# Moving the casts and remainders of a three-way bf16 split to other steps of a software-pipelined attention kernel

## The chip, the cores and the metric

One core of one Trainium2 chip runs the whole kernel. The metric is the device time in microseconds (us); three runs gave 420.11, 420.8 and 423.27, median 420.8.

## What is computed

The input `x` is 8 batches of 512 tokens with 128 features. One transformer layer is applied:

```
x = layernorm(x + attention(x))          # 16 heads of 8 features, causal
x = layernorm(x + channel_mix(x))
# scores of one head, before the softmax
scores = alpha * tanh(q @ k.T / beta) + lam * (soft_bits @ soft_bits.T) / 2 \
         + (hexc @ M_h @ hexc.T) / 6 * 2 * sigmoid(scale)
soft_bits, hexc = tanh(x @ hex_w.T), tanh(x @ q6_w.T)      # 6 features each
# channel_mix: r = sigmoid(mix_r @ W_r.T); out = r * (relu(mix_k @ W_k.T)**2 @ W_v.T)
```

The products that make the scores run on TensorE in bf16. To keep float32 accuracy, each of their operands is split into three bf16 levels whose sum is the float32 value.

## The kernel before

**Periods and steps.** Work is written out by hand in periods, one for each batch `b`, and each period has 20 steps `t`. One step handles a pair of 128x512 score blocks. Five engines each have their own instruction list with the same steps, and they meet only at semaphores. For pair `t`, TensorE makes the raw scores (`scores`, L513), ScalarE takes the tanh (`tanh`, L777), TensorE adds the bias product (`biases`, L538), VectorE adds the two (`main`, L999, one step later), ScalarE takes the exponential three steps later (`exp`, L786), GpSimd zeroes what lies above the diagonal (`mask`, L882), and TensorE multiplies with the values (`weighted`, L557, at steps given by `VALUES_STEPS`). PSUM holds three pairs, so `scores(t)` waits until `main(t-3)` is done. I write main(9) for `main` of pair 9, which is VectorE's first instruction in step 10; mask(6) is `mask` of pair 6, GpSimd's first in step 9.

**Side work.** Within period `b`, two further batches are served. "Post" finishes batch `b-1`: normalising the attention output, the output projection, residual and layernorm, the channel mix and its layernorm. "Prep" makes the stacks of batch `b+2`: the transposed input, the projections Q and K, the features J (`feats`, made by ScalarE) and the mapped features G. The dictionaries `PREP` and `POST` of VectorE (L1113) and GpSimd (L935) say in which step each stage stands. An engine does its main instruction first, then the stages of `PREP`, then those of `POST`. Period 0 has prep and no post, periods 1 to 5 have both, periods 6 and 7 have post alone. What comes ahead of period 0 is written out separately.

**The split.** For each of Q, K, J, G, four instructions follow one another across two engines: `hi` (VectorE casts the float32 value to bf16, level 0), `rest` (GpSimd subtracts level 0), `mid` (VectorE casts the remainder, level 1), and `lo` (GpSimd subtracts level 1 and writes level 2). All work on tiles of 128x512. After `lo`, the SyncE queue writes the three levels to DRAM (`to_dram`, in the order Q, K, J, G, each after its own `lo`), and in the next period loads them back as stacks (`load_stacks`). `hi` of the next batch overwrites level 0 in `parts`, so it waits until the DRAM write of the batch before has landed (`scr_in`, L1037).

**The first layernorm of the post work.** In step 10 VectorE adds the residual (L1101), takes statistics (L1089) and moments (L1096). GpSimd then makes the inverse deviation in its step 10 (`inv_std`, L913 and L915) and normalises in step 11 (`norm`, L923 and L927). In between stands mask(8). TensorE's `weighted(7)` in step 13 needs mask(8), and its transpose of the normalised tile in step 14 (L598) needs `norm`.

Of the kernel before, what the change touches and what calls it, by code (L numbers as in the profile page):

```python
# [62 lines left out]
Q, K, J, G = range(4)  # L63
# [76 lines left out]
def build(nc, x, qkv_w, out_w, hex_w, lam_logit, q6_w, transforms, transform_weights, scale_logit,  # L140
# [17 lines left out]
    with ExitStack() as ctx:  # L158
# [181 lines left out]
        def lagged(b, t, lag):  # L340

            return (b, t - lag) if t >= lag else (b - 1, t - lag + PAIRS)
# [8 lines left out]
        def _(sp):  # L351
# [150 lines left out]
            for half, (_, bs, _) in enumerate(HALVES):  # L502
                sp.wait_ge(tail["final"], half + 1)
                sp.dma_start(out[B - 1].rearrange("(n p) c -> p n c", p=P)[:, bs], final[:, bs]).then_inc(stored, 16)
# [4 lines left out]
        def _(pe):  # L509
# [232 lines left out]
            for half, (blocks, _, _) in enumerate(HALVES):  # L742
                pe.wait_ge(tail["sums"], half + 1)
                transposes(tail_bank("sums_T", half), lambda n: sums_sb[:, 1, n * P:(n + 1) * P],
                           blocks).then_inc(tail["sums_T"], 1)
            for half, (blocks, _, _) in enumerate(HALVES):
                pe.wait_ge(tail["attn_first"], 1)
                pe.wait_ge(tail["attn"], half + 1)
                transposes(tail_bank("attn_T", half), lambda n: attn[:, n, :], blocks).then_inc(tail["attn_T"], 1)
# [118 lines left out]
        def _(pool):  # L868
# [13 lines left out]
            def mask(b, t):  # L882

                v, p = pair_probs(t), t % PAIRS_PER_QUAD
                if p < 4:
                    blocks = [v[:, :, 0:P]] + ([v[:, :, 3 * P:T]] if p >= 2 else [])
                else:
                    blocks = [v.rearrange("p u (r i) -> p (u r) i", r=2)[:, :, 0:P]]
                pool.wait_ge(exp_done, PAIRS * b + t + 1)
                stand_alone(pool)  # L890
                for v in blocks:
                    last = nc.gpsimd.affine_select(out=v, in_=v, compare_op=ALU.is_ge, fill=0.0, base=0,  # L892
                                                   pattern=[[0, v.shape[1]], [1, P]], channel_multiplier=-1)
                last.then_inc(mask_done, 1)
# [35 lines left out]
            def gated_residual(n):  # L930
# [1 line left out]
                pool.wait_ge(dve_freed, side_units.through(n + 1, "kv"))  # L932
                nc.gpsimd.tensor_tensor(res[:], gated[:], x1[:], ALU.add).then_inc(gate_done, 1)

            PREP = {6: [(rest, Q)], 10: [(lo, Q), (rest, K)], 13: [(lo, K), (rest, J)], 14: [(rest, G)],  # L935
                    16: [(lo, J)], 17: [(lo, G)]}
            POST = {10: [(inv_std, 0)], 11: [(norm, 0)], 18: [(gated_residual,)], 19: [(inv_std, 1), (norm, 1)]}

            def period(b, par, post, prep, last=False):
                for t in range(PAIRS):  # L940
                    if t >= EXP_LAG or post:
                        mask(*lagged(b, t, EXP_LAG))
                    for stage, *a in PREP.get(t, []) if prep else []:
                        stage(b + 2, *a)
# [40 lines left out]
        def _(dve):  # L985
# [78 lines left out]
            def sums_out(n, k):  # L1064

                dve.wait_ge(pv_done, PAIRS * n + (k + 1) * PAIRS // 2)
                v.tensor_copy(sums_sb[:, k, :], sums[:]).then_inc(sums_read, 1)
# [38 lines left out]
            def gate(n):  # L1106
# [3 lines left out]
                v.scalar_tensor_tensor(out=gated[:], in0=r_tanh[:], scalar=1.0, in1=o, op0=ALU.add,  # L1110
                                       op1=ALU.mult).then_inc(dve_freed, 1)

            PREP = {0: [(x_out,)], 2: [(projected, Q)], 3: [(projected, K)], 5: [(hi, Q)], 9: [(mid, Q), (hi, K)],  # L1113
                    11: [(mid, K), (hi, J)], 12: [(features_i,)], 13: [(hi, G)], 15: [(mid, J)], 17: [(mid, G)]}
            POST = {1: [(normalise, 0)], 6: [(normalise, 1)], 8: [(attn_out,)],
                    10: [(residual,), (stats, 0, 0), (stats, 0, 1), (moments, 0)], 14: [(x1_out,)],
                    18: [(gate,)], 19: [(stats, 1, 0), (stats, 1, 1), (moments, 1)]}
# [1 line left out]
            def period(b, par, post, prep, values=True):  # L1119
                parity[0] = par  # L1120
                for t in range(PAIRS):
# [4 lines left out]
                    if t == VALUES_STEPS[PAIRS // 2 - 1]:  # L1126
                        sums_out(b, 0)
                    for stage, *a in PREP.get(t, []) if prep else []:
                        stage(b + 2, *a)
# [230 lines left out]
```

## Time and profile before

| | |
|---|---|
| median of three runs | 420.8 us |
| profiled execution, its own time | 420.74 us |
| span of its trace | 418.8 us |
| mean granted TensorE clock | 0.985 |
| busy: PE, VectorE (DVE), ScalarE (ACT), GpSimd (POOL) | 368.2, 332.7, 327.3, 230.6 us |
| busy share of the span | 88%, 79%, 78%, 55% |
| VectorE `main` (L1004), 160 instructions | 202.8 us, mean 1274 ns |
| GpSimd `rest` (L899) and `lo` (L905) together, 60 instructions | 70.9 us |
| VectorE `hi` (L1038) and `mid` (L1043) together, 64 instructions | 36.5 us |

The busy shares are averages over the whole span. All four engines are well used, so what counts is which of them is waited for in which step. The trace is therefore read period by period. Period 3 of the kernel runs from about 175 to 219 us from the span's start, and periods 1 to 5 repeat nearly to the hundredth of a microsecond.

### The profile page before, as it was taken

To read this page: it belongs to the slowest core of one execution; us is meant where nothing else is said; L and a number is where in the kernel's file an instruction comes from. 1 tells how busy PE (TensorE), PEld (TensorE's weight loads), DVE (VectorE), ACT (ScalarE), POOL (GpSimd) and SP (SyncE) were. 2 spreads that over 40 slices of the span, in tenths; PEclk is the share of its full clock that TensorE was granted. 3 is DMA by queue.
4 is the path that set the end of the run, shared out by engine and by line. 5 is a ranking of instruction groups with operands and counts; after the bars stand their busy time and mean duration, and the time that the engine had idled before them with its cause. 6 is when DMAs were issued, how large, how long until landed. Compare 5 with 4: busy or idle time off the path is not lost.

```text
span 418.8 us, 8760 instructions
## 1 busy us (share of the span) xinstructions
PE 368.2 (88%) x2907; PEld 191.3 (46%) x2907; DVE 332.7 (79%) x539; ACT 327.3 (78%) x364; POOL 230.6 (55%) x367
## 2 busy tenths in 40 slices
PE   4557798899999999999899989999989998999863
PEld 1232343345455544645364535454544554345442
DVE  4873677988988989798979897989887958786643
ACT  1002389999998989799889989899989998999621
POOL 4313535834687359644965488646873446344532
PEclk9999999999999999999999999999999999899978
DMA  3354587786621775167624764276318610100000
GB/s 100 94 144 121 162 275 189 232 236 166 200 84 48 205 193 172 49 164 195 190 80 121 188 182 131 85 194 186 123 52 206 173 59 7 45 27 1 2 27 25
DMA packets 37807, 53.74 MB, mean 128 GB/s; under 512 B 3522, under 2 KB 35266, under 8 KB 36190
## 3 DMA queue, kind: packets, MB, share of 16 engines
q1 hardware_dynamic: 34078, 51.49, 43.4%
q10 hardware_dynamic: 3696, 1.84, 1.8%
q8 instruction: 18, 0.29, 0.3%
q14 instruction: 15, 0.12, 0.1%
HBM read 38.69 MB, written 14.61 MB: 127 GB/s over the span
## 4 chain that ended last, share of the span: by engine, by line
PE 50%; DVE 15%; issue 10%; POOL 9%; SPq 7%; ACT 5%; DMA 3%; ACTq 1%; POOLq 0%; DVEq 0%
PE raw L511 22%; PE side_bank L511 13%; PE sums L511 12%; DVE probs L1004 6%; ACT probs L788 3%; PE side_bank L598 3%; POOL probs L892 2%; SPq L401 2%; ACT probs L783 2%; POOL x L927 2%; POOL x L923 2%; SPq L415 2%; POOL parts L905 2%; SPq L412 2%; DVE bn L1089 1%
## 5 line engine op out<-in xcount | busy, mean ns | idle before, releaser
L1004 DVE SCALAR_TENSOR_TENSOR probs<-probs,scal,raw 128x1024 f32<-128x1024 f32 x160 | 202.8, 1274 | 40.4 <-PE raw L511 39.4
L783 ACT ACTIVATE probs<-raw 128x1024 f32<-128x1024 f32 x160 | 163.9, 1025 | 33.2 <-PE raw L511 32.2
L892 POOL TENSOR_SCALAR_AFFINE_SELECT probs<-probs 128x256 f32<-128x256 f32 (+1 forms) x224 | 98.9, 458 | 131.6 <-ACT probs L788 131.1
L788 ACT ACTIVATE probs<-probs 128x1024 f32<-128x1024 f32 x160 | 169.3, 1060 | 0.9 <-DVE probs L1004 0.9
L511 PE MATMUL raw<-q_stack,k_stack 72*128 72x384 bf16 (+3 forms) x512 | 99.0, 306 | 10.9 <-DVE probs L1004 6.9
L511 PE MATMUL raw<-i_stack,j_stack 111*128 111x384 bf16 (+3 forms) x512 | 98.1, 304 | 2.7 <-ACT probs L783 2.5
L511 PE MATMUL sums<-probs,values 128*32 128x256 f32 (+2 forms) x1280 | 93.3, 391 | 5.1 <-POOL probs L892 4.1
L511 PEld LDWEIGHTS raw<-q_stack,k_stack 72*128 72x128 bf16 x512 | 38.9, 99 | 63.8 <-DVE probs L1004 35.3
L511 PEld LDWEIGHTS raw<-i_stack,j_stack 111*128 111x128 bf16 x512 | 42.4, 99 | 48.6 <-issue 15.3
L511 PEld LDWEIGHTS sums<-probs,values 128*32 128x32 f32 x1280 | 29.8, 109 | 50.9 <-issue 27.2
L899 POOL TENSOR_TENSOR whole<-whole,parts 128x512 f32<-128x512 f32 x22 | 26.2, 1189 | 23.1 <-DVE parts L1038 23.1
L905 POOL TENSOR_TENSOR parts<-whole,parts 128x512 bf16<-128x512 f32 x30 | 35.1, 1171 | 4.2 <-DVE parts L1043 4.2
L1043 DVE CAST parts<-whole 128x512 bf16<-128x512 f32 x32 | 19.6, 612 | 2.9 <-POOL whole L899 2.8
L915 POOL TENSOR_TENSOR rstd<-var_eps,minus_half 128x4 f32<-128x4 f32 x14 | 14.7, 1047 | 1.2
L796 ACT ACTIVATE feats<-side_bank 128x512 f32<-128x512 f32 x8 | 4.9, 611 | 12.4 <-PE side_bank L511 12.4
L511 PEld LDWEIGHTS side_bank<-w_r_mix,x1T 128*128 128x128 f32 x112 | 13.6, 191 | 1.0
L511 PE MATMUL side_bank<-w_r_mix,x1T 128*128 128x128 f32 x112 | 13.6, 275 | 0.0
L511 PE MATMUL side_bank<-x1T,w_k_mix 128*128 128x512 f32 x28 | 13.2, 591 | 0.0
L835 ACT ACTIVATE probs<-shift_col 1x1536 bf16<-1x1536 bf16 x1 | 1.5, 1481 | 14.6 <-DVE w_r_mix L1244 14.6
L1038 DVE CAST parts<-whole 128x512 bf16<-128x512 f32 x24 | 12.3, 511 | 0.7 <-DMA q_rows<-parts 0.5
L1089 DVE BATCH_NORM_STATS2 bn<-res 128x6 f32<-128x128 f32 x56 | 12.2, 280 | 0.2
L511 PE MATMUL side_bank<-xT,wqT 128*128 128x512 f32 x14 | 9.7, 781 | 2.9 <-DVE xT L1019 2.3
(144 smaller groups left out, 347.6 us busy)
## 6 DMA issues: line engine op xcount, KB each, us to landing
q_stack<-q_rows SPq DMA_DIRECT2D x21, 384.0 KB
k_stack<-k_rows SPq DMA_DIRECT2D x21, 384.0 KB
i_stack<-lattice_i SPq DMA_DIRECT2D x21, 288.0 KB
i_stack<-hamming_i SPq DMA_DIRECT2D x21, 288.0 KB
q_rows<-parts SPq DMA_DIRECT2D x8, 384.0 KB, 8.7
k_rows<-parts SPq DMA_DIRECT2D x8, 384.0 KB, 3.0
lattice_i<-parts SPq DMA_DIRECT2D x8, 288.0 KB
k_rows<-parts SPq DMA_DIRECT2D x8, 256.0 KB, 3.3
```

The lines of the kernel that those rows point to most:

```text
L511: return nc.tensor.matmul(o, lhsT, rhs, start=start, stop=stop, **kw)
L598: last = nc.tensor.transpose(o[:, n * P:(n + 1) * P], src(n), ident[:])
L783: nc.scalar.activation(pair_probs(t), raw[:, t % PSUM_PAIRS, :].rearrange("p (u i) -> p u i", u=2), ACT.Tanh).then_inc(tanh_done, 1)
L788: nc.scalar.activation(pair_probs(t), pair_probs(t), ACT.Exp).then_inc(exp_done, 1)
L892: last = nc.gpsimd.affine_select(out=v, in_=v, compare_op=ALU.is_ge, fill=0.0, base=0, pattern=[[0, v.shape[1]], [1, P]], channel_multipli ...
L899: nc.gpsimd.tensor_tensor(whole[:, kind, :], feats[:] if kind == J else whole[:, kind, :], parts[:, kind, 0, :], ALU.subtract).then_inc(re ...
L905: nc.gpsimd.tensor_tensor(parts[:, kind, 2, :], whole[:, kind, :], parts[:, kind, 1, :], ALU.subtract).then_inc(lo_done[kind], 1)
L915: nc.gpsimd.tensor_tensor(rstd[:], var_eps[:], minus_half[:], ALU.pow).then_inc(rstd_done, 1)
L1004: v.scalar_tensor_tensor(out=o, in0=o, scalar=scal[:, 2:3], in1=raw[:, t % PSUM_PAIRS, :].rearrange("p (u i) -> p u i", u=2), op0=ALU.mult ...
L1038: v.tensor_copy(parts[:, kind, 0, :], feats[:] if kind == J else whole[:, kind, :]).then_inc(hi_done[kind], 1)
L1043: v.tensor_copy(parts[:, kind, 1, :], whole[:, kind, :]).then_inc(mid_done[kind], 1)
L1089: v.bn_stats(bn[:, blk, :], res[:, blk, :]).then_inc(bn_done, 1)
```

## The change

Nothing is added or taken out. Some stages stand at other steps. `hi` of K goes from step 9 to 5, of J from 11 to 6, of Q from 5 to 4. `mid` of Q goes from 9 to 8, of K from 11 to 9, of J from 15 to 12, of G from 17 to 16. On GpSimd `rest` of Q goes from 6 to 5, of K from 10 to 6, of J from 13 to 8; `lo` of Q from 10 to 9, of J from 16 to 14.

```diff
-            PREP = {6: [(rest, Q)], 10: [(lo, Q), (rest, K)], 13: [(lo, K), (rest, J)], 14: [(rest, G)],
-                    16: [(lo, J)], 17: [(lo, G)]}
+            PREP = {5: [(rest, Q)], 6: [(rest, K)], 8: [(rest, J)], 9: [(lo, Q)], 13: [(lo, K)],
+                    14: [(lo, J), (rest, G)], 17: [(lo, G)]}
...
-            PREP = {0: [(x_out,)], 2: [(projected, Q)], 3: [(projected, K)], 5: [(hi, Q)], 9: [(mid, Q), (hi, K)],
-                    11: [(mid, K), (hi, J)], 12: [(features_i,)], 13: [(hi, G)], 15: [(mid, J)], 17: [(mid, G)]}
+            PREP = {0: [(x_out,)], 2: [(projected, Q)], 3: [(projected, K)], 4: [(hi, Q)], 5: [(hi, K)], 6: [(hi, J)],
+                    8: [(mid, Q)], 9: [(mid, K)], 12: [(features_i,), (mid, J)], 13: [(hi, G)], 16: [(mid, G)]}
```

The code ahead of period 0 has its own order of the same stages and is left as it is.

## Rows read from the trace of the kernel before

**Rows 1.** The chain that ended last, whole span: start, us, what.

```profile
113.73 1.03 POOL x L923
291.72 1.02 POOL x L923
376.18 1.02 POOL x L923
```

**Rows 2.** Timeline of PE, 178 to 226 us: start, us, what, idle before.

```profile
201.37 0.61 PE L511 MATMUL raw<-q_stack,k_stack 72*128 72x384 bf16 x4 [0.41 <-DVE probs L1004]
...
202.98 0.85 PE L511 MATMUL sums<-probs,values 128*32 128x384 f32 x8 [0.56 <-POOL probs L892]
...
205.27 0.63 PE L598 MATMUL side_bank<-ident,x 128*128 128x128 f32 x4 [0.46 <-POOL x L927]
...
206.19 0.60 PE L511 MATMUL raw<-q_stack,k_stack 72*128 72x512 bf16 x2
```

**Rows 3.** Timeline of GpSimd (POOL), same stretch.

```profile
193.45 0.41 POOL L892 TENSOR_SCALAR_AFFINE_SELECT probs<-probs 128x256 f32<-128x256 f32 x1 [1.22 <-ACT probs L788]
195.97 0.66 POOL L892 TENSOR_SCALAR_AFFINE_SELECT probs<-probs 128x256 f32<-128x256 f32 x1 [2.11 <-ACT probs L788]
...
198.57 1.16 POOL L905 TENSOR_TENSOR parts<-whole,parts 128x512 bf16<-128x512 f32 x1
...
200.81 0.24 POOL L913 TENSOR_SCALAR var_eps<-mean_var 128x4 f32<-128x4 f32 x1
...
208.85 1.16 POOL L899 TENSOR_TENSOR whole<-whole,parts 128x512 f32<-128x512 f32 x1
209.97 1.67 POOL L892 TENSOR_SCALAR_AFFINE_SELECT probs<-probs 128x256 f32<-128x256 f32 x4
...
219.97 0.23 POOL L913 TENSOR_SCALAR var_eps<-mean_var 128x4 f32<-128x4 f32 x1 [1.21 <-DVE mean_var L1096]
```

**Rows 4.** Timeline of VectorE (DVE), same stretch.

```profile
185.15 1.28 DVE L1004 SCALAR_TENSOR_TENSOR probs<-probs,scal,raw 128x1024 f32<-128x1024 f32 x1 [0.32 <-PE raw L511]
...
192.96 1.28 DVE L1004 SCALAR_TENSOR_TENSOR probs<-probs,scal,raw 128x1024 f32<-128x1024 f32 x1 [1.00 <-PE raw L511]
...
194.75 1.27 DVE L1004 SCALAR_TENSOR_TENSOR probs<-probs,scal,raw 128x1024 f32<-128x1024 f32 x1
195.94 0.42 DVE L1043 CAST parts<-whole 128x512 bf16<-128x512 f32 x1
196.28 0.63 DVE L1038 CAST parts<-whole 128x512 bf16<-128x512 f32 x1
196.83 1.26 DVE L1004 SCALAR_TENSOR_TENSOR probs<-probs,scal,raw 128x1024 f32<-128x1024 f32 x1
...
199.75 0.38 DVE L1096 BATCH_NORM_AGGREGATE mean_var<-bn 128x2 f32<-128x6 f32 x4 [0.15 <-DVE bn L1089]
...
209.07 1.22 DVE L1043 CAST parts<-whole 128x512 bf16<-128x512 f32 x1
210.21 1.27 DVE L1004 SCALAR_TENSOR_TENSOR probs<-probs,scal,raw 128x1024 f32<-128x1024 f32 x1
...
219.39 0.38 DVE L1096 BATCH_NORM_AGGREGATE mean_var<-bn 128x2 f32<-128x6 f32 x4 [0.15 <-DVE bn L1089]
```

**Rows 5.** Timeline of all engines, 17.3 to 19 us, ahead of period 0.

```profile
17.43 1.15 POOL L905 TENSOR_TENSOR parts<-whole,parts 128x512 bf16<-128x512 f32 x1 [1.01 <-DVE parts L1043]
17.45 1.41 DVE L1038 CAST parts<-feats 128x512 bf16<-128x512 f32 x1
```

**Rows 6.** Timelines of SyncE (SP) and VectorE, 46 to 92 us: period 0.

```profile
54.57 0.90 SPq L384 DMA_DIRECT2D k_rows<-parts  x1
...
58.55 0.49 DVE L1038 CAST parts<-whole 128x512 bf16<-128x512 f32 x1 [0.49 <-DMA q_rows<-parts]
```

**Rows 7.** DMA issues, 50 to 64 us: KB, median us to landing.

```profile
k_rows<-parts SPq DMA_DIRECT2D x1, 256.0 KB, 5.6
```

**Rows 8.** Timeline of PE in period 0, 46 to 92 us.

```profile
78.76 0.64 PE L511 MATMUL sums<-probs,values 128*32 128x256 f32 x8 [0.84 <-DVE sums_sb L1067]
```

## The prediction, made before the changed kernel was run

> **What bounds the kernel now.** I read the chain that ended last first, for the length of a period. The first layernorm of a batch begins at 113.73 us in period 1, at 291.72 in period 5 and at 376.18 in period 7 [rows 1]. So a period with prep lasts (291.72 - 113.73) / 4 = 44.5 us and one without it (376.18 - 291.72) / 2 = 42.2 us. The last two have no prep at all, so the five periods 1 to 5 pay 2.3 us each for having it, 11 us in all. Moving prep stages can hardly win more than part of that.
>
> Next I read TensorE's timeline of one period, for its idle time. There are three waits in steps 12 to 14, and the reader should see who ends each: 0.41 us for a `main` of VectorE, 0.56 for mask(8) of GpSimd, 0.46 for the normalised tile of GpSimd [rows 2]. From 205.27 to 219 us TensorE runs without a wait. So what matters in periods 1 to 5 is when VectorE and GpSimd get through steps 8 to 11.
>
> Last I read these two engines there. GpSimd does lo Q at 198.57 and rest K behind it, and only at 200.81 the first part of `inv_std`, although the moments it needs were ready at 199.75 + 0.38 = 200.13 [rows 3, 4]. After a wait for moments, 0.20 us pass (219.39 + 0.38 = 219.77 to 219.97) [rows 3, 4]. So GpSimd's own backlog costs the layernorm 200.81 - 200.33 = 0.48 us, and mask(8) and the normalised tile are late by as much.
>
> **How casts and GpSimd collide.** A cast on VectorE alone takes 0.42 us (195.94). Where GpSimd is in the middle of an instruction of its own, the cast is held up: at 209.07 one took 1.22 us beside a subtraction that ran from 208.85 to 210.01, and VectorE's next instruction began at 210.21, 0.20 us after GpSimd's end [rows 3, 4]. The other way round, mask(6) took 0.66 instead of 0.41 us, since a cast had begun 0.03 us before it [rows 3, 4]. A tie goes to the earlier one: GpSimd began at 17.43, the cast at 17.45, and the cast took 1.41 us [rows 5].
>
> **The change part by part, periods 1 to 5.**
>
> 1. hi Q moves to step 4, ahead of main(4). That `main` now waits 0.32 us for TensorE [rows 4]. The cast issues 0.34 us before its successor (195.94 to 196.28), so the cost is 0.02 at most, taken as nothing. hi K takes the place that hi Q had in step 5. It comes while GpSimd's mask is in progress, as hi Q's cast did; rest Q moves behind it and has until the next mask. Nothing.
> 2. hi J is new in step 6. At worst it is held up like the second cast of rows 4 (0.63 us). main(7) later waits 1.00 us for TensorE [rows 4], which covers it. rest K takes rest Q's place on GpSimd. Nothing. If that cover were gone it would cost 0.3 to 0.6 us a period.
> 3. mid Q comes to step 8, just when GpSimd does rest J, also new there. mask(5) begins at 193.45 and takes 0.41; the next instruction is shown 0.04 before its forerunner's end (208.85 + 1.16 = 210.01 against 209.97) [rows 3]. So rest J runs from 193.82 to 194.98. mid Q is due at 194.75, the place that main(8) has now [rows 4], and is held up; main(8) begins at 194.98 + 0.20 = 195.18, 0.43 later than before.
> 4. mid K comes to step 9, in place of mid Q and hi K. It is due 1.19 us after main(8) (194.75 to 195.94), at 196.37. lo Q, now in step 9 too, follows mask(6), which nothing lengthens any more: 195.97 + 0.41 - 0.04 = 196.34. lo Q is first by 0.03 us. I take it that it wins, as GpSimd did in rows 5 with 0.02. It lasts 1.16, to 197.50, and main(9) begins at 197.70 instead of 196.83 [rows 4]: 0.87 us later. The two bounds are 0.87 later and, if mid K goes first, 196.37 + 0.34 = 196.71, 0.12 earlier. I take the upper one by the nearest row.
> 5. TensorE reaches `scores(12)` and `scores(13)` as late as main(9) and main(10) let it. Residual, statistics and moments follow main(9), so the moments end at 200.13 + 0.87 = 201.00 and `inv_std` starts at 201.20. GpSimd is free then, since lo Q and rest K are gone from step 10. Against 200.81 this is 0.39 later, and so are mask(8) and `norm`. Its lateness of 0.87 at `scores(13)` meets the wait of 0.56 for mask(8) [rows 2] and a mask that is 0.39 late: 0.87 is less than 0.56 + 0.39, so the mask still comes last, and TensorE goes on 0.39 late, at the transpose as well.
> 6. The rest gives relief where nobody waits. Taking mid K and hi J out of step 11 frees 0.67 us, mid J's 1.22 us go from step 15, and rest J goes from GpSimd's step 13. But TensorE is never idle behind 205.27 until the period's end. mid J in step 12 meets `norm` and waits for it, up to 0.6 us, which the 0.67 cover.
> 7. On the SyncE queue, J's write to DRAM is issued earlier, behind K's as before; the writes of Q, K and G keep their order. Level 0 is overwritten earlier, but in the next period, some 20 us after those writes. Nothing.
>
> Sum for five periods: 5 x 0.39 = 2.0 us slower.
>
> **Period 0.** hi Q waits here for the DRAM write of the batch before: the cast began only at 58.55 after 0.49 us of idle time [rows 6]. In step 4 it waits for the same landing, so main(4), which now stands ahead of it and began at 58.55 - 0.49 - 1.28 = 56.78, begins at 58.55 + 0.42 = 58.97: 2.2 us later. hi K behind it waits for K's write, 54.57 + 5.6 = 60.2 [rows 6, 7]. Later this period has slack to give back: mid K no longer waits for GpSimd, and TensorE's 0.84 us at 78.76 for VectorE [rows 8] can go. Bounds: 2.2 slower, 0.8 faster. I take 0.3 slower, nearer to the side where gaps are given back, since TensorE meets several short gaps in steps 13 to 16.
>
> **Sum.** The profiled execution took 420.74 us (span 418.8 and 1.9 around it), which stands 0.1 under the median of 420.8. 420.74 + 2.0 + 0.3 = 423.0.
>
> A rule of the Trainium skill bears on the tie. Its page "SBUF — State Buffer", section "SBUF: two separate sides", says that the port pair which VectorE and GpSimd share is an exclusive lock: whichever instruction starts first keeps it to its end. By that rule lo Q, 0.03 us ahead, shuts mid K out and the sum is 423.0; if the start that counts is not the recorded one, the same rule gives 418.0, as in rival A. The trace agrees that it is no sharing of bandwidth (1.22 against 0.42 us).
>
> **Rivals.**
>
> A. *mid K gets in ahead of lo Q.* In rows 3 and 4 the cast that had waited since 209.07 went ahead of masks recorded from 209.97, before the subtraction had ended at 210.01. So GpSimd's recorded start is not yet its hold. If mid K, due at 196.37, is counted as waiting when mask(6) ends at 196.38, it goes first. Then main(9) is 0.12 early, the moments end at 200.01, `inv_std` starts at 200.21 and all behind it is 0.60 earlier: 5 x 0.60 = 3.0 faster, with period 0 420.74 - 3.0 + 0.3 = 418.0. For it: a margin of 0.03 us between two times that I worked out. Against it: rows 5.
>
> B. *VectorE falls behind a second time.* mid J, new in step 12, is due at about 203.9 (the new main(10) begins at 200.9, then two `main` of 1.19 each and a copy). `norm`'s two instructions of 1.02 us [rows 1] end just ahead of the transpose, which comes at 205.27 + 0.39 = 205.66, so they run from about 203.4 to 205.5. If mid J is held through both instead of the first alone, main(12) begins at 205.7 and ends at 207.0. scores(15) needs it, and TensorE would be there at 206.19 + 0.39 = 206.6 [rows 2]: another 0.4 lost. 5 x (0.39 + 0.4) = 4.0, and 420.74 + 4.0 + 0.3 = 425.0, slower. It decides once main(12) begins after 206.6 - 1.3 = 205.3. For it: two GpSimd instructions back to back just there. Against it: at 209.97 a waiting cast got in between two of them [rows 3, 4].
>
> C. *The order hardly matters.* The gaps are filled by other work or hi's new waits are nil, and periods 0 to 5 come out within 1 us in all: 420 to 422. For it: three of four engines have slack in most steps. Against it: the three waits are the only ones in steps 10 to 19.
>
> **How the numbers follow.** Forecast 0.45, A 0.27, C 0.15, B 0.13. The predicted time is 423.0. The range starts at A with the lower bound of period 0, 418.0 - 1.1 = 416.9, and ends at the forecast with period 0's upper bound, 423.0 + 1.9 = 424.9; about half of B and the far tails stay out. About 1% (4.2 us) is what a measurement of this kernel can tell from no change. Faster by more needs under 416.6: a tail of A, 0.13. Slower by more needs over 425.0: B for the most part, 0.12. Within 1%: 0.75.
>
> **What would show it.** In the trace of the changed kernel, period 3: mid K at about 196.4 takes 1.4 us (0.42 by rival A) and lo Q stands beside it; main(9) begins 0.87 later than before against main(7); the first part of `inv_std` has an idle time before it, ended by the moments; periods 1 to 5 last 44.9 us (43.9 by A, 45.3 by B). In period 0, a wait of hi Q for the landing of about 0.5 to 1.7 us and one of hi K. I am wrong if TensorE shows new waits in steps 5 to 9, where I costed three moved casts at nothing, or if the waits of rows 2 are gone and the period is still no shorter.

## The result, and the profile after

| | before | changed |
|---|---|---|
| median | 421.9 us (6 runs) | 427.7 us (6 runs, 426.7 to 429.1) |
| ratio to before, 95% interval | 1 | 1.0132 [1.0094, 1.0169] |
| profiled execution, its own time | 420.74 us | 427.75 us |
| span of its trace | 418.8 us | 425.8 us |
| mean granted TensorE clock | 0.985 | 0.973 |

The change makes the kernel 5.8 us slower. 423.0 had been predicted, with a range up to 424.9, so it is slower by two and a half times as much as forecast.

The chain that ended last gives the lengths of the periods, by the first layernorm of each, as in [rows 1]. It is the whole span of the changed kernel: start, us, what.

```profile
116.76 1.02 POOL x L923
...
297.17 1.02 POOL x L923
...
340.63 1.02 POOL x L923
...
383.12 1.02 POOL x L923
```

From period 1 to period 5 a period lasts (297.17 - 116.76) / 4 = 45.10 us, against 44.50: 0.60 more. The single periods are not alike to the hundredth of a microsecond: in the traces they last 44.33, 44.86, 44.33 and 44.47 before, and 44.97, 45.43, 44.96 and 45.05 now. Each is 0.57 to 0.64 longer, so period 3 can stand for all. From 297.17 to 340.63 there are 43.46 us, against 42.02 between the same two instructions before (291.72 to 333.74):

```profile
333.74 1.02 POOL x L923
```

The last stretch, 42.49, is as before (42.44). The start of a period can also be read from VectorE's copy of the transposed input (L1019). It begins at 46.92 and 87.26 before, so period 0 lasts 40.34. Now the two are:

```profile
47.37 0.68 DVE L1019 COPY xT<-side_bank 128x512 f32<-128x512 f32 x1
...
89.71 0.68 DVE L1019 COPY xT<-side_bank 128x512 f32<-128x512 f32 x1
```

Period 0 lasts 42.34, which is 2.0 more. So the 7.0 us between the two profiled executions are 0.45 ahead of period 0, where nothing was changed; 2.0 in period 0; 5 x 0.60 = 3.0 in periods 1 to 5; and the last 1.5 behind them, where nothing was changed either. The sections below take these apart.

**Periods 1 to 5.** Here is VectorE in period 3, the stretch that answers to [rows 4] (start, us, what, idle before).

```profile
192.64 0.42 DVE L1038 CAST parts<-feats 128x512 bf16<-128x512 f32 x1
...
193.36 0.42 DVE L1075 TENSOR_TENSOR x<-side_bank,den_inv 128x256 f32<-128x256 f32 x1
...
196.79 1.28 DVE L1004 SCALAR_TENSOR_TENSOR probs<-probs,scal,raw 128x1024 f32<-128x1024 f32 x1 [1.00 <-PE raw L511]
197.99 0.95 DVE L1043 CAST parts<-whole 128x512 bf16<-128x512 f32 x1
198.86 0.68 DVE L1080 COPY attnT<-side_bank 128x512 f32<-128x512 f32 x1
199.46 1.26 DVE L1004 SCALAR_TENSOR_TENSOR probs<-probs,scal,raw 128x1024 f32<-128x1024 f32 x1
200.65 0.98 DVE L1043 CAST parts<-whole 128x512 bf16<-128x512 f32 x1
201.55 1.27 DVE L1004 SCALAR_TENSOR_TENSOR probs<-probs,scal,raw 128x1024 f32<-128x1024 f32 x1
...
204.47 0.38 DVE L1096 BATCH_NORM_AGGREGATE mean_var<-bn 128x2 f32<-128x6 f32 x4 [0.15 <-DVE bn L1089]
```

GpSimd beside it, answering to [rows 3]:

```profile
197.49 1.16 POOL L899 TENSOR_TENSOR whole<-feats,parts 128x512 f32<-128x512 f32 x1
199.81 0.41 POOL L892 TENSOR_SCALAR_AFFINE_SELECT probs<-probs 128x256 f32<-128x256 f32 x1 [1.15 <-ACT probs L788]
200.18 1.16 POOL L905 TENSOR_TENSOR parts<-whole,parts 128x512 bf16<-128x512 f32 x1
...
205.05 0.23 POOL L913 TENSOR_SCALAR var_eps<-mean_var 128x4 f32<-128x4 f32 x1 [2.62 <-DVE mean_var L1096]
```

Both casts are held up: mid Q (197.99) takes 0.95 us beside rest J, mid K (200.65) takes 0.98 beside lo Q, where 0.42 is a cast's time alone. The pair of them makes main(9) begin 201.55 - 196.79 = 4.76 after main(7), against 196.83 - 192.96 = 3.87 before: 0.89 later. GpSimd is now idle for 2.62 us until the moments come. From main(7) to the first part of `inv_std` it takes 205.05 - 196.79 = 8.26 us, against 200.81 - 192.96 = 7.85: 0.41 later, once in each of these periods. The other 0.60 - 0.41 = 0.19 is lost ahead of main(7).

TensorE in the same period, answering to [rows 2]:

```profile
193.28 0.60 PE L511 MATMUL raw<-q_stack,k_stack 72*128 72x384 bf16 x4
193.84 1.16 PE L511 MATMUL side_bank<-wvT,xT 128*128 128x128 f32 x8
...
206.08 0.61 PE L511 MATMUL raw<-q_stack,k_stack 72*128 72x384 bf16 x4 [0.74 <-DVE probs L1004]
...
207.21 0.85 PE L511 MATMUL sums<-probs,values 128*32 128x384 f32 x8
...
209.50 0.63 PE L598 MATMUL side_bank<-ident,x 128*128 128x128 f32 x4 [0.46 <-POOL x L927]
```

The wait for VectorE has grown from 0.41 to 0.74, the wait for the mask is gone (the mask ends at 207.15, as TensorE gets there at 207.13), and the one for the normalised tile is 0.46 as before. TensorE is still not idle behind it.

**Period 0.** VectorE and TensorE, answering to [rows 6]; then, in windows of 2 us, busy time of PE, weight load, VectorE, ScalarE and GpSimd with their instructions, the granted clock, the DMA share and GB/s.

```profile
58.76 0.43 DVE L1038 CAST parts<-whole 128x512 bf16<-128x512 f32 x1 [4.06 <-DMA q_rows<-parts]
```

```profile
60.43 1.03 PE L511 MATMUL raw<-q_stack,k_stack 72*128 72x384 bf16 x4 [4.04 <-DVE probs L1004]
```

```profile
58.00:60.00 2.00, 0.00 (x0) 0.00 (x0) 1.24 (x2) 0.01 (x1) 0.73 (x1) 0.58 1.03 323
60.00:62.00 2.00, 1.57 (x6) 0.64 (x6) 1.93 (x3) 0.50 (x1) 2.00 (x4) 0.50 0.83 229
62.00:64.00 2.00, 2.00 (x9) 1.36 (x9) 1.93 (x3) 2.00 (x3) 0.82 (x2) 0.50 0.77 221
```

hi Q now waits 4.06 us for the landing, main(4) stands behind it (59.10 to 60.37), and TensorE is idle for 4.04 us. Its granted clock falls to 0.50, which is 1.2 GHz, in that stop, and behind it a group of matmuls that takes 0.61 elsewhere takes 1.03.

### The profile page after: what moved, and what is told of

It is laid out like the page before. It is cut to its first block, busy times and chain, and to the rows that moved or that the text cites. A ratio compares the mean times of both kernels' runs of the same rounds, so it can differ in the third digit from the quotient of the medians.

```text
span 425.8 us, 8760 instructions
## 1 busy us (share of the span) xinstructions
PE 372.2 (87%) x2907; PEld 191.5 (45%) x2907; DVE 334.6 (79%) x539; ACT 327.6 (77%) x364; POOL 230.3 (54%) x367
## 3 DMA queue, kind: packets, MB, share of 16 engines
q1 hardware_dynamic: 34078, 51.49, 42.6%
## 4 chain that ended last, share of the span: by engine, by line
PE 49%; DVE 17%; issue 9%; SPq 8%; POOL 6%; ACT 6%; DMA 3%; POOLq 0%; DVEq 0%; ACTq 0%
PE raw L511 21%; PE side_bank L511 13%; PE sums L511 11%; DVE probs L1004 6%; ACT probs L783 4%; PE side_bank L598 3%; ACT probs L788 2%; SPq L401 2%; DVE bn L1089 2%; DMA q_stack<-q_rows 2%; POOL x L927 2%; POOL x L923 2%; SPq L415 2%; SPq L412 2%; POOL probs L892 1%
## 5 line engine op out<-in xcount | busy, mean ns | idle before, releaser
L892 POOL TENSOR_SCALAR_AFFINE_SELECT probs<-probs 128x256 f32<-128x256 f32 (+1 forms) x224 | 97.5, 452 | 122.7 <-ACT probs L788 121.5
L1043 DVE CAST parts<-whole 128x512 bf16<-128x512 f32 x32 | 22.4, 700 | 1.1 <-POOL whole L899 1.0
L915 POOL TENSOR_TENSOR rstd<-var_eps,minus_half 128x4 f32<-128x4 f32 x14 | 14.7, 1047 | 1.2
L913 POOL TENSOR_SCALAR var_eps<-mean_var 128x4 f32<-128x4 f32 x14 | 3.2, 230 | 22.2 <-DVE mean_var L1096 22.2
L1038 DVE CAST parts<-whole 128x512 bf16<-128x512 f32 x24 | 11.8, 493 | 4.3 <-DMA q_rows<-parts 4.1
L835 ACT ACTIVATE probs<-shift_col 1x1536 bf16<-1x1536 bf16 x1 | 1.5, 1481 | 14.6 <-DVE w_r_mix L1244 14.6
```

The source lines that it names most:

```text
L915: nc.gpsimd.tensor_tensor(rstd[:], var_eps[:], minus_half[:], ALU.pow).then_inc(rstd_done, 1)
L1038: v.tensor_copy(parts[:, kind, 0, :], feats[:] if kind == J else whole[:, kind, :]).then_inc(hi_done[kind], 1)
L1043: v.tensor_copy(parts[:, kind, 1, :], whole[:, kind, :]).then_inc(mid_done[kind], 1)
```

## The experiments

All timed ratios are to the kernel before. Edits are against the changed kernel unless it is said otherwise. The runs of before that they are compared with had a median of 421.6 us for the first four, 420.8 for the rest. Where an edit adds lines, the line numbers in the rows of its trace are higher: L1043 with early rows is the `hi` of L1038.

**Which part costs what: period 0 by itself.** In the first kernel, period 0 takes its steps from the old dictionaries, on both engines. The second is the reverse: the kernel before, with the new dictionaries in period 0 alone.

```diff
+            PREP_0 = {... the dictionary of before ...}
...
-                    for stage, *a in PREP.get(t, []) if prep else []:
+                    for stage, *a in (PREP_0 if isinstance(b, int) and b == 0 else PREP).get(t, []) if prep else []:
```

> The changed kernel, but period 0 keeps the old steps on both engines. Theory: in period 0 hi Q stands ahead of main(4) and waits 4.06 us for the landing of the DRAM write of the batch before, and TensorE stands still for 4.04 us; period 0 as a whole costs 2.0 us (first normalise instruction of period 1 against the end of the code ahead of period 0). Then this kernel takes 427.7 - 2.0 = 425.7 us, its period 0 is as in the kernel before, and TensorE's wait of 4 us and its slow matmuls behind it are gone. Rival (the wait is given back later, as I forecast): 427.4 us, since then period 0 was worth 0.3.

> The kernel before, but period 0 has the new steps on both engines. Theory: 421.9 + 2.0 = 423.9 us, with the wait of 4 us in period 0 and periods 1 to 5 of 44.5 us. Rival (period 0 nearly neutral): 422.2 us.

Measured: with the old period 0, 424.4 us, ratio 1.0073 [1.0034, 1.0113]; with the new one alone, 425.3, 1.0105 [1.0046, 1.0164]. In the traces period 0 lasts 86.84 - 46.70 = 40.14 and 89.84 - 47.40 = 42.44 us, and periods 1 to 5 last 45.09 and 44.48: each part appears where its dictionary was used, and nowhere else. Against before the steady part costs 2.8 us by the medians and the new period 0 3.6. Neither alone accounts for the 5.8; their sum is 6.4, and the intervals of the two are 1.7 and 2.5 us either way. Period 0 thus costs more than the 2.0 that both expectations took from the profiled pair, in which it had 42.34 and 40.34.

**hi J behind the normalising.** In step 6 the cast of J's features stood ahead of `normalise`, which frees the side bank that TensorE needs for the values (`wvT`). Here it follows.

```diff
-            PREP = {... 5: [(hi, K)], 6: [(hi, J)], ...
+            PREP = {... 5: [(hi, K)], ...
+            LATE = {6: [(hi, J)]}
...
+                    for stage, *a in LATE.get(t, []) if prep else []:
+                        stage(b + 2, *a)
```

> The changed kernel, but hi of J stands behind the normalisation in step 6 on VectorE, not ahead of it. Theory: ahead of it, the cast keeps the one side bank of PSUM occupied 0.34 us longer, the value projection of step 7 (v1) starts 0.2 us late and so does all that follows; without that periods 1 to 5 last 44.9 instead of 45.1 us, v1 follows scores(8) with no gap, and the time is 427.7 - 1.0 = 426.7 us. Rival (the 0.2 us per period come from the collisions of casts in steps 8 and 9 alone, 0.6 together): periods stay at 45.1 us and the time at 427.7.

Measured: 426.2 us, 1.0127 [1.0070, 1.0183]; a period lasts (296.87 - 117.30) / 4 = 44.89. TensorE, period 3:

```profile
193.57 0.60 PE L511 MATMUL raw<-q_stack,k_stack 72*128 72x384 bf16 x4
194.01 1.11 PE L511 MATMUL side_bank<-wvT,xT 128*128 128x128 f32 x8
```

The same two groups in the kernel before:

```profile
189.61 0.60 PE L511 MATMUL raw<-q_stack,k_stack 72*128 72x384 bf16 x4
190.05 1.11 PE L511 MATMUL side_bank<-wvT,xT 128*128 128x128 f32 x8
```

The values' matmuls begin 0.44 after the scores ahead of them in both, and take 1.11. In the changed kernel it is 0.56, and they take 1.16: there `normalise` ends only at 193.36 + 0.42 = 193.78, and they begin at 193.84. The period gets back 0.21, which is the 0.19 that was lost ahead of main(7). The total doesn't tell this version from the changed one; the period length and the row do.

**lo Q behind the layernorm's adds.** Only GpSimd's lo Q goes back, from step 9 to 10.

```diff
-            PREP = {5: [(rest, Q)], 6: [(rest, K)], 8: [(rest, J)], 9: [(lo, Q)], 13: [(lo, K)],
+            PREP = {5: [(rest, Q)], 6: [(rest, K)], 8: [(rest, J)], 10: [(lo, Q)], 13: [(lo, K)],
```

> The changed kernel, but lo of Q stands in step 10 of GpSimd again, where GpSimd idles 2.6 us ahead of inv_std. Theory: mid K in step 9 is shut out by lo Q (0.98 to 1.05 us instead of 0.42), which makes main(9), the moments, inv_std and the transpose late; with lo Q gone from there mid K takes 0.42 us, inv_std comes 0.57 us earlier against main(7), periods 1 to 5 last 44.5 us, and the time is 427.7 - 2.9 = 424.8 us. Rival (the first collision, mid Q with rest J in step 8, decides and the second only follows): mid K's relief is used up by TensorE, which is late from step 8 on, and the periods stay above 45.0 us, the time above 427.

Measured: 424.7 us, 1.0078 [1.0046, 1.0110]; a period lasts (294.09 - 116.21) / 4 = 44.47. VectorE and GpSimd, period 3:

```profile
199.43 0.41 DVE L1043 CAST parts<-whole 128x512 bf16<-128x512 f32 x1
```

```profile
201.19 1.16 POOL L905 TENSOR_TENSOR parts<-whole,parts 128x512 bf16<-128x512 f32 x1
203.28 0.23 POOL L913 TENSOR_SCALAR var_eps<-mean_var 128x4 f32<-128x4 f32 x1 [0.93 <-DVE mean_var L1096]
```

With lo Q out of its way mid K takes 0.41 instead of 0.98, and the period is 0.63 shorter: as short as before the change, though mid Q is still held up. The medians fell by 3.0 us, which agrees with 5 x 0.63. What this kernel is still slower than before, 3.1 us by the medians, is then period 0.

**The rows of batch 1 written earlier.** The wait of period 0 is for a DRAM write, so this experiment moves the write. SyncE's list ahead of period 0 ended with it; now it stands behind the loads of Q and K.

```diff
-                for kind in (Q, K, G):
+                for kind in (Q, K):
...
-                write_rows(1, 1)
+                for kind in (Q, K, J):
+                    sp.wait_ge(lo_done[kind], 2)
+                    to_dram(kind, 1)
+                load_stack(G, 0, stack_in[G], (8, H))
+                sp.wait_ge(lo_done[G], 2)
+                to_dram(G, 1)
```

> The changed kernel, all steps as in it, but ahead of period 0 the SyncE queue writes the split rows of batch 1 (Q, K, J) to DRAM before the last G loads, so about 5 us earlier. Theory: hi Q in step 4 of period 0 then finds its write landed, VectorE's wait of 4.06 us and TensorE's of 4.04 us are gone, period 0 (from its x_out to the next) lasts 40 instead of 42.3 us, and the time is 427.7 - 2.0 = 425.7 us or less. Rival (moving stages at all, not the landing, makes period 0 long): it stays at 42 us and the time at 427.7.

Measured: 424.9 us, 1.0102 [1.0051, 1.0153]. The queue issues Q's write at 48.76, against 54.14 in the changed kernel, and hi Q no longer waits. SyncE, VectorE's hi Q, and the window in which TensorE had stood still:

```profile
48.76 0.52 SPq L380 DMA_DIRECT2D q_rows<-parts  x1
```

```profile
56.43 0.42 DVE L1043 CAST parts<-whole 128x512 bf16<-128x512 f32 x1
```

```profile
56.00:60.00 4.00, 3.73 (x23) 1.14 (x22) 4.00 (x7) 4.00 (x6) 2.14 (x4) 1.00 0.63 182
```

Period 0 lasts 86.51 - 46.93 = 39.58 us, 2.8 less than in the changed kernel and 0.8 less than before, and the granted clock stays at 1.00. Periods 1 to 5 keep their 45.09. So the wait for the landing is the cause of period 0's loss, and not the places of the casts as such.

**rest J one step earlier.** Everything as in the changed kernel, save that rest J stands in step 7, so that mid Q in step 8 meets an idle GpSimd.

```diff
-            PREP = {5: [(rest, Q)], 6: [(rest, K)], 8: [(rest, J)], 9: [(lo, Q)], 13: [(lo, K)],
+            PREP = {5: [(rest, Q)], 6: [(rest, K)], 7: [(rest, J)], 9: [(lo, Q)], 13: [(lo, K)],
```

> The changed kernel, but rest of J stands in step 7 of GpSimd instead of 8. Theory: mid Q in step 8 is no longer shut out by rest J (0.42 instead of 0.95 us), main(8) starts 0.5 us earlier, and mid K is then due while mask(6) runs, just ahead of lo Q. If the cast that waits goes ahead of GpSimd's next instruction (my rival A), mid K takes about 0.5 us and periods 1 to 5 last 44.5 us, 427.7 - 3 = 424.7 us in all; if lo Q still wins, mid K takes over 1.2 us, the periods 45.0 to 45.1 us and the time 427.4.

Measured: 421.7 us, 1.0006 [0.9971, 1.0040]; a period lasts (292.72 - 116.75) / 4 = 43.99. VectorE, then GpSimd, period 3:

```profile
196.86 0.42 DVE L1043 CAST parts<-whole 128x512 bf16<-128x512 f32 x1
...
198.99 0.42 DVE L1043 CAST parts<-whole 128x512 bf16<-128x512 f32 x1
199.32 1.27 DVE L1004 SCALAR_TENSOR_TENSOR probs<-probs,scal,raw 128x1024 f32<-128x1024 f32 x1
```

```profile
198.68 0.41 POOL L892 TENSOR_SCALAR_AFFINE_SELECT probs<-probs 128x256 f32<-128x256 f32 x1 [2.27 <-ACT probs L788]
199.05 1.38 POOL L905 TENSOR_TENSOR parts<-whole,parts 128x512 bf16<-128x512 f32 x1
```

This one step takes away 6.0 us by the medians, 5 x 1.11 = 5.6 of them in the length of the periods, where 3 had been expected. It is more than the steady part had lost: a period is now 0.51 shorter than before, and that stands against a period 0 that is still long (43.39 us here). The step gains twice over. mid Q takes 0.42 instead of 0.95. mid K, due 0.53 earlier for that, arrives while mask(6) is in progress (198.68 to 199.09), and goes ahead of lo Q: the cast takes 0.42, and lo Q is stretched to 1.38.

This comes near the encounter that the prediction weighed as a tie, and it ends as in rival A. It doesn't show rival A's reason, though. mid K is recorded 0.06 us ahead of lo Q, where the tie had it 0.03 behind, so "the earlier recorded start goes first" gives the same. The two rules differ only for a cast recorded after GpSimd's next instruction has begun and before the one ahead of it has ended. By the single instructions of the traces, three casts come to that narrow place, each between two masks. Two went first (80.25 in the second trace of before, 80.05 in the version with the old period 0 below): they are recorded 0.02 us before the first mask's end and level with the second's start. One lost and took 0.64 us (55.77 in the version with early rows below): it is recorded 0.01 before the first mask's end and 0.04 after the second's start. The prediction's tie, 0.01 before and 0.03 after, is nearest to the one that lost. So rival A's rule does not hold down to the last 0.01 us, and what would have become of the tie stays open.

**Steps built from what was found.** rest J in step 7, lo Q in step 10, hi J and mid Q behind the post work of steps 6 and 8, and the old steps in period 0.

```diff
-            PREP = {5: [(rest, Q)], 6: [(rest, K)], 8: [(rest, J)], 9: [(lo, Q)], 13: [(lo, K)],
+            PREP = {5: [(rest, Q)], 6: [(rest, K)], 7: [(rest, J)], 10: [(lo, Q)], 13: [(lo, K)],
...
-            PREP = {... 5: [(hi, K)], 6: [(hi, J)], 8: [(mid, Q)], 9: [(mid, K)], ...
+            PREP = {... 5: [(hi, K)], 9: [(mid, K)], ...
+            LATE = {6: [(hi, J)], 8: [(mid, Q)]}
```

> The changed kernel with what theory says hurts taken out: old steps in period 0; from period 1 on rest J in step 7, lo Q in step 10, hi J behind the normalisation in step 6, mid Q behind the attention output in step 8. Theory: no cast is shut out by a subtraction ahead of the moments, v1 is not held up, inv_std waits for the moments alone, and they come earlier than in the kernel before: periods 1 to 5 last 44.0 us (44.5 before), period 0 40.3, and the time is 421.9 - 2.5 = 419.4 us, a ratio of 0.994. Rival (VectorE's work ahead of step 10 is more than before, so its moments come no earlier): 44.4 us a period and 421.5 us.

Measured: 418.8 us, 0.9935 [0.9898, 0.9972]. A period lasts (289.73 - 114.56) / 4 = 43.79, 0.71 less than before. The idle time of GpSimd ahead of `inv_std` is down to 0.41 us (200.24), so the engine is late for nothing and waits for little. Its period 0 is longer than the 40.3 expected: 41.82 us in the old order, with hi Q waiting 3.03 us.

**The same steps in every period, with and without the early rows.** The first adds the SyncE order of the earlier experiment to these steps; the second leaves that order as in the changed kernel.

> As the kernel before this one in the list, but period 0 has the same new steps too, and the rows of batch 1 are written to DRAM early. Theory: with the landing out of the way period 0 gains as well, since mid K no longer waits for GpSimd there: 39.5 us instead of 40.3, and the time is 0.8 us under that of e7, 418.6 us. Rival (the G stacks of batch 0, loaded later now, are missed by TensorE in step 11 of period 0): a wait for that DMA and a time over that of e7.

> The mended steps (rest J in 7, lo Q in 10, hi J and mid Q behind the post stages) in every period, period 0 too, with the old order of the SyncE queue. Theory: periods 1 to 5 of 43.8 us as in e7, but period 0 of 42.3 us or more, since hi Q ahead of main(4) waits for its landing as in the changed kernel: 418.8 + 1.5 = 420.3 us or a little less. Rival (the early rows of e8 gave nothing, the steps did): 417.8 us as e8.

Measured: 417.8 us, 0.9909 [0.9881, 0.9937] with the early rows, and 421.3, 1.0008 [0.9979, 1.0038] without. The first has the lowest median found, 3.0 us under before and 9.9 under the changed kernel; from the version with the old period 0 (418.8) its interval does not tell it. The two differ in the order of one queue and by 3.5 us; the new steps in period 0 without that order eat up the gain of the steady part (421.3 against 418.8 with the old period 0). The early rows were not run with the steps of the kernel before, so how much of the 3.0 us that order alone would give is not known. What limits this version next is again a transfer, the wait that the rival had foreseen, though at the start of period 1 and not in period 0. TensorE in its profiled execution:

```profile
88.38 0.85 PE L516 MATMUL raw<-i_stack,j_stack 111*128 111x512 bf16 x2 [3.86 <-DMA i_stack<-hamming_i]
```

Period 0 lasts 83.77 - 46.92 = 36.85 us, but the next one, by the same copy of VectorE, 49.32, where it is 43.73 with the old period 0. So in this execution all of period 0's gain against that version is handed back: its layernorm of period 1 begins at 115.11 us, against 114.53. This execution took 421.0 us, the longest of the eleven; that the others wait less there is likely but not shown.

**Both kernels once more.** One execution of each, to see what of the profiled pair repeats.

> The changed kernel once more, for a second trace. Theory: what the steps do repeats to 0.1 us (periods 1 to 5 of 45.1 us, TensorE's wait of about 4 us in period 0 for hi Q's landing, v1 late by 0.2), while the stretches in periods 6 and 7 at a granted clock of 0.5 are not of the change and may be there or not (1.4 and 1.1 us each). Rival (they belong to the change): both again at the same places.

> The kernel before once more, for a second trace. Theory: periods 1 to 5 of 44.5 us again; period 0 between 40.1 and 41.9 us, by whether TensorE runs slow matmuls (1.03 instead of 0.6 us for a group) ahead of hi Q or waits for its landing instead; stretches at 0.5 in periods 6 and 7 may be there or not. Rival (they belong to the change): none in period 6.

Measured: 425.26 us for the changed kernel, 421.68 for the one before. Periods 1 to 5 last (296.94 - 116.59) / 4 = 45.09 and (293.36 - 115.45) / 4 = 44.48, so they repeat to 0.02. What does not repeat is period 0 of the kernel before. Here is its second trace, VectorE and TensorE, and then TensorE in the changed kernel's second trace:

```profile
58.64 0.55 DVE L1038 CAST parts<-whole 128x512 bf16<-128x512 f32 x1 [2.77 <-DMA q_rows<-parts]
```

```profile
60.43 0.61 PE L511 MATMUL raw<-q_stack,k_stack 72*128 72x384 bf16 x4 [2.73 <-DVE probs L1004]
```

```profile
60.25 1.04 PE L511 MATMUL raw<-q_stack,k_stack 72*128 72x384 bf16 x4 [3.82 <-DVE probs L1004]
```

hi Q waits 2.77 us in the old order too, where the first trace had 0.49 [rows 6]. The landing comes at the same time in both (58.55 and 58.64). The difference is how far TensorE and VectorE had got by then. In the first trace the groups of matmuls from 48.85 to 53.4 took 1.03 to 1.06 us, in the second 0.61:

```profile
48.85 1.03 PE L511 MATMUL raw<-q_stack,k_stack 72*128 72x384 bf16 x4 [1.32 <-DVE probs L1004]
```

```profile
49.27 0.61 PE L511 MATMUL raw<-q_stack,k_stack 72*128 72x384 bf16 x4 [1.31 <-DVE probs L1004]
```

The 0.49 was therefore no measure of the slack, the time by which hi Q could come earlier at no cost. What stands still at a landing is what arrives early, and the faster start of the second run only turned into a longer wait. Period 0 lasted 41.64 us in this run of before and 42.13 in that of the changed kernel: 0.5 apart, and the whole 3.6 us between these two executions are 0.5 + 5 x 0.61.

## Why the prediction was wrong

**Steps 3 to 5, the stretch around the layernorm, were right in size, in part by luck.** The forecast had main(9) 0.87 later against main(7), `inv_std` 0.39 later and waiting for the moments. The trace has 0.89 (196.79 to 201.55 against 192.96 to 196.83), 0.41, and a wait of 2.62 us for the moments. That both casts are shut out is what was expected, and taking away either collision gives back more than the 0.41: 0.63 a period with lo Q moved, 1.11 with rest J moved. Step 5 had the mask end TensorE's wait; mask and TensorE came within 0.02 us of each other instead, and the lateness of 0.4 was the same.

**Two sizes inside these steps were wrong, and they cancelled.** `PREP` stages stand ahead of `POST` ones in a step. So mid Q comes ahead of the copy `attn_out`, while step 3 put it behind, at the place of main(8). It is due at 197.99, half a microsecond after rest J began, and takes 0.95. main(8) comes 199.46 - 196.79 = 2.67 after main(7), against 194.75 - 192.96 = 1.79 before: 0.88 later where 0.43 had been forecast. From main(8) to main(9) it is 2.09, as before (2.08), where 0.44 more had been forecast, because mid K did not come within 0.03 us of lo Q. It came 200.65 - 200.18 = 0.47 behind it. There was no tie, and the chances that I gave to its two outcomes went to an encounter that did not happen. That the total of steps 3 to 5 came out right is therefore luck. A cast waiting at the end of mask(6) was met in the kernel with rest J in step 7, and it went first; that a period lasts 43.99 us there, against the 43.9 named for A, is a coincidence, since mid Q is not held up in that kernel and the 0.19 of step 2 is still lost.

The Trainium skill says on its page "SBUF — State Buffer", section "SBUF: two separate sides", that the port pair which VectorE and GpSimd share is an exclusive lock, kept by whichever starts first for its whole instruction. The traces agree: mid K ends at 201.63, 0.29 after lo Q (200.18 + 1.16 = 201.34). What they add is that a cast recorded while GpSimd's instruction before is still in progress counts as first, as the row at 198.99 shows.

**Step 2, "Nothing", failed.** I had asked whether hi J would make main(7) late and found it covered by main(7)'s wait of 1.00. That wait is still 1.00 (196.79), since the lateness goes through TensorE. hi J stands ahead of `normalise`, `normalise` frees the side bank, TensorE's values wait for that bank, and its scores stand behind the values in its list. What is late is the work that main(7) waits for, so its wait covers nothing. That cost of nothing is the step of the prediction whose mechanism failed. It costs 0.19 a period, 1.0 us in all; putting hi J behind `normalise` gave back 0.21.

**Period 0 failed in size: 0.3 was taken, 2.0 is what the profiled pair shows, and about 3 what the medians show.** This is the term that was furthest off. It had the right mechanism, and a bound of 2.2 on its sum: main(4) behind a cast that waits for a landing. Two reasons for choosing 0.3 did not carry. The first was that gaps later in the period would give the time back. They gave back 0.8 us in sum: the gap of 0.84 shrank to 0.21, and gaps of 0.62 (73.52 before) and 0.39 (75.31) went, but another of 0.82 for ScalarE came at 83.51, where before there was 0.24:

```profile
80.61 0.64 PE L511 MATMUL sums<-probs,values 128*32 128x256 f32 x8 [0.21 <-DVE sums_sb L1067]
...
83.51 0.61 PE L511 MATMUL raw<-i_stack,j_stack 111*128 111x384 bf16 x4 [0.82 <-ACT probs L783]
```

The second was that the wait of 0.49 stood for the kernel. It did not: the wait was short because TensorE had been slow just before. And the longer stop brought a cost with it that no row of before could have told, the clock at 1.2 GHz for about 5 us behind it.

How much period 0 costs depends on the pace of TensorE just ahead of the wait, and the profiled pair mixes two paces. From about 49 us on, the groups of matmuls take 0.61 us in some traces, whichever the steps, and up to 1.06 for 3 to 6 us in others. Period 0 in all traces with the old order of the queue, sorted by that:

| TensorE behind 48.5 us | old steps in period 0 | new steps in period 0 |
|---|---|---|
| groups of 0.61 us | 41.64, 41.82 | 42.34, 42.13 |
| slow for 3 to 6 us | 40.34, 40.14 | 42.44, 43.27, 43.09, 43.39, 43.37 |

At the fast pace the new steps cost 0.5 us in the means, at the slow one 2.9. The 2.0 of the profiled pair compares a slow trace of before (40.34) with a fast one of the changed kernel (42.34). At the slow pace hi Q in its old place nearly meets its landing (waits of 0.49 and 1.52 us), and the clock stays at 1.00. In its new place hi Q makes TensorE stand still for 1.4 to 2.9 us, and a stretch at a granted clock of 0.5 follows, until after 66 us in three of the five. The medians less the lengths of periods 1 to 5 leave 2.6 to 4.0 us for period 0, over the six kernels with its new steps and the old queue, and 2.9 with the 3.0 of the steady part makes up the 5.8. So most executions were presumably at the slow pace, but runs without a trace don't say which they had.

**Steps 6 and 7 and rival B.** mid J in step 12 takes 0.71 us (207.74) and delays nobody: TensorE is not idle behind 209.50. `norm` (207.12) and mid J collided as thought, but it cost the cast only 0.71 - 0.42 = 0.29. B's second backlog did not occur, though its total, 425.0, lies nearer to the result than mine. The time it named would have been right for another reason.

**The sum and the range.** 2.0 + 0.3 had been forecast. What was found is 2.0 for steps 3 to 5, 1.0 for step 2 and about 2.9 for period 0, at the pace that fits the medians. The upper end of the range was the steady forecast with period 0's upper bound, 1.9 more. It had no room for an edit that was costed at nothing and would cost 0.3 to 0.6 a period by my own words in step 2. 5 x 0.3 on top of 424.9 gives 426.4, and 5 x 0.6 gives 427.9. Only with the 0.6 would the range have held 427.7, and then by luck: step 2 itself took 0.19, and the rest was period 0 beyond its bound.

**The 1.5 us behind period 5 are not of the change.** In periods 6 and 7 the two kernels do the same. In windows of 4 us, the changed kernel has two stretches with a low granted clock there, and before had one:

```profile
320.00:324.00 4.00, 3.50 (x19) 0.98 (x18) 2.05 (x2) 4.00 (x5) 1.33 (x3) 0.64 0.88 239
364.00:368.00 4.00, 3.53 (x22) 1.21 (x26) 1.88 (x3) 4.00 (x6) 1.12 (x3) 0.69 0.17 48
```

```profile
358.00:362.00 4.00, 4.00 (x32) 1.36 (x30) 2.17 (x2) 4.00 (x5) 0.82 (x2) 0.57 0.02 4
```

The second trace of the kernel before has its stretch at 316 to 321 us, and then its interval between the fifth and sixth layernorm is 336.56 - 293.36 = 43.20 where the first had 42.02, and the next is 41.38 where the first had 42.44. The second trace of the changed kernel has one stretch alone, at 320 to 324. The other traces agree. Where the first of these intervals holds no such stretch, it lasts 42.00 to 42.02 us, with the steps of before as with the new ones (early rows, hi J behind). Where it holds one, it lasts 43.20 to 43.49, and the 43.49 belongs to the kernel with the steps of before in periods 1 to 5. The second interval is 41.37 without a stretch and 42.4 to 42.6 with one; it is 43.9 once, with a longer one. A stretch of this length thus costs 1.1 to 1.5 us, wherever it falls. The 42.2 us that the prediction gave a period without prep held one as well.

## What to carry to other kernels

A cost of nothing is a claim about everybody who waits for the engine, and not only about the next instruction on it. Ask for each stage that is put ahead of another what that other one frees, and for whom; and when a cost of nothing rests on a cover, put the price without the cover into the range. Where two engines exclude each other, move the pair apart by a step and not the single instruction: one remainder moved by one step was worth 5 x 1.11 us here, 6 by the medians. A wait for a landing that is short in one trace may only say that the waiting side was slow that time, as here; its bound is what would be waited for if that side were fast, and the cure is an earlier transfer.

## What the runs showed of the hardware

- **The clock can fall in a stop of TensorE, and the stop is then paid for afterwards as well.** In the 4.04 us of standing still before 60.43 the granted clock went from 1.00 to 0.50 and was 0.50 until after 64 us. Groups of 0.61 took 1.03 to 1.06. Behind a stop of 1.24 us at the same place, in the trace with the old period 0, it stayed at 1.00. The Trainium skill's page "TensorE: Matmul & The Clock Gate", section "Part 1: The HAM clock gate (the "warmup" mystery)", says that the clock is halved after the engine was idle, and the row of the 4.04 us agrees.
- **It falls in busy stretches as well.** Ahead of 320 to 324 us TensorE was never idle for more than 0.56 us at a time, and the clock still went to 0.50 for some 3 us. It fell behind two waits of TensorE for ScalarE, of 0.56 and 0.50 us. The first trace of before has the same two waits at 313.39 and 315.25 and no fall behind them, and again at 355.72 and 357.58, where it fell. What decides was not tested.
- **A clock of 1.00 ahead of a trace's first clock record is no reading.** From 48.85 to 53.4 us of the first trace of before, groups took 1.03 to 1.06 as they do at 1.2 GHz, while the view says 1.00:

```profile
50.00:52.00 2.00, 2.00 (x5) 0.61 (x5) 0.27 (x1) 1.89 (x2) 0.00 (x0) 1.00 0.68 205
```

  The trace holds no clock record before 54.66 us, and the views fill that with 1.00. Where the records begin differs from trace to trace: at 14.6 us in the one of the kernel with the old period 0. From 20 to 40 us these two do the same work in the same busy time, and the views say 1.00 and 0.50. So their mean granted clocks (0.985 and 0.956) can't be compared; the durations of the same group can.

```profile
20.00:40.00 20.00, 12.81 (x29) 5.65 (x28) 11.94 (x35) 1.48 (x1) 4.19 (x5) 1.00 0.49 145
20.00:40.00 20.00, 12.80 (x29) 5.65 (x28) 11.95 (x35) 1.48 (x1) 4.18 (x5) 0.50 0.49 146
```

- **Who gets the shared pair.** A cast that is held up by a subtraction or a mask of GpSimd ends 0.28 to 0.29 us after that instruction (201.63 after 201.34, 196.91 after 196.63). One that is recorded 0.06 us or more before GpSimd's next instruction goes ahead of that one, though the instruction in progress may end later (198.99 with 0.42, beside lo Q from 199.05 with 1.38). One recorded 0.02 us or more after GpSimd's start loses (17.45 with 1.41). A cast beside the power of `inv_std` on 128x4 (L915, 201.13 to 202.18 before) was not held up: at 201.23 it took 0.42.
